# First causal attention of a four-layer kernel: where the row maximum gets its mask, and when the query and key stacks are turned and copied

## The chip, the cores and the metric

One core of one Trainium2 chip runs the whole program. The metric is the device time of one launch in microseconds (us), the median of several runs. Engines: PE (TensorE), DVE (VectorE), ACT (ScalarE), POOL (GpSimd), SP (DMA issue).

## The reference, cut to what matters

Four layers, each followed by a layer norm over 4 x 512 tokens of width 256. The change is in the first one alone:

```
Q = (x @ Wq.T).reshape(b, h, t, d)          # b 4, h 16, t 512, d 16
K = (x @ Wk.T).reshape(b, h, t, d)
V = (x @ Wv.T).reshape(b, h, t, d)
scores = einsum('bhqd,bhkd->bhqk', Q, K)
scores = where(causal, -inf, scores)        # causal: k > q
weights = softmax(scores / sqrt(d))
ctx = einsum('bhqk,bhkd->bhqd', weights, V) # then @ Wp.T + bp, + x, layer norm
```

Behind it come a gated mixture of eight experts, a second attention with 16 heads of width 128, and a routed feed-forward layer.

## The kernel before, in words

**Slots, groups, chunks.** The 64 heads (4 x 16) of the first attention are worked in 16 groups of four heads. A group `g` has two slots, `p = 2g` (even, `j = 0`) and `p = 2g + 1` (odd, `j = 1`), and a slot handles a pair of heads, one on partitions 0 to 63 and one on 64 to 127. Each engine walks the same list of slots (`l0_slot`, from -6 to 33), and each slot has three chunks. The order of the work on an engine is the order in which its `l0_slot` calls the helpers; semaphores tie the engines together. Nothing is planned at run time.

**Two passes over the scores.** The softmax needs the row maximum before the exponential. In the first pass (`l0_scores`, two slots ahead) PE multiplies queries by keys with query rows on the partitions, into banks 0 (first head) and 1 (second head), and DVE takes the row maximum of each row tile (`l0_maxima`, L1405 to L1416) into `nm0`. Chunk 0 is the row tile with 512 keys, chunk 1 the tiles with 384 and 128 keys in one bank, chunk 2 the tile with 256 keys; each for both heads. POOL splits the maxima into three bf16 parts (`l0_split_maxima`, L1925 to L1928), and PE folds them into the queries (`l0_row_maxima`, L544 and L547). In the second pass (`l0_turned_scores`, L563 the mask and L568 the scores, banks 3 to 5) the scores come out with the keys on the partitions and the maximum already taken off; ACT exponentiates them from PSUM (`l0_exponentials`, L1082), and PE multiplies by the values (`l0_context`, L584, bank 6), turns the result back (`l0_context_turns`, L593), and DVE copies it out (L1401).

**The mask of the first pass.** PE writes it: before the scores of a row tile, four 64-row matmuls (L526), two per head, put the 128 x 128 causal triangle (0 or -1e30, as identity times mask) on the diagonal block, and the score matmul (L531) adds to it. The first of them for a head waits on `a["max"]` until DVE has read what that bank held before.

**The stacks.** PE projects a group's queries and keys three groups ahead (`l0_project`, even slot, chunk 2, L457 to L459) and its values (`l0_values`, odd slot, chunk 2). ACT and DVE split queries and keys into bf16 parts (`l0_parts_high`, even slot, chunk 2; `l0_parts_low`, odd slot, chunk 0, L1356), POOL writes duplicates (L1893). Then PE turns both, one after the other, through bank 7: 32 transposes of 64 x 64 each (`l0_stack`, L507). The turned queries are copied to SBUF by ACT (`l0_q_stack`, L1063, a 128 x 1024 copy), the turned keys by DVE (`l0_k_stack`, L1384 to L1390, the same size). The turns of the keys wait for ACT's copy of the queries (`a["stq"]`), the next turns of queries for DVE's copy of the keys (`a["stk"]`). In the kernel before, the query turns are in chunk 1 of the even slot, the key turns in chunk 1 of the odd slot; ACT's copy is in chunk 1 of the even slot, DVE's in chunk 1 of the odd slot.

**The early work.** From slot 26 on, the tables `EARLY_AT` put the first steps of the next layer (`cc`, `first`, `join`, `norm`, `x1`) between the attention's own. Their turns (`turn_mix`, L648) use bank 7 too, so PE waits there for the stacks' copies.

`mask` is a 128 x 512 tile of constants: zeros, and the triangle in its last 128 columns, so that `mask[:, 512 - w:512]` is the mask of a row tile with `w` keys. The second attention's first pass already uses it in this way (`maxima`, L1418 to L1429): one DVE instruction adds the mask to the scores in PSUM, writes the sum to SBUF and takes the row extreme, and a second one reads the accumulator out.

Of the kernel before, what the change touches and what calls it, by code (L numbers as in the profile page):

```python
# [7 lines left out]
ALU = mybir.AluOpType  # L8
# [3 lines left out]
P = 128  # L12
# [134 lines left out]
def build(nc, x_tok_d, x_t_d, wqkv_d, wall_d, const_d, bp_d, outb_d, b2_d, rb_d, eb_d, rw0_d, rw1_d, b1_d, out_d):  # L147
    ctx = ExitStack()
    with ctx:
# [304 lines left out]
        def _(pe):  # L454
# [35 lines left out]
            def l0_stack(g, which):  # L490

                tok = (q_tok, k_tok)[which][g % 2]
                hold(pe, m["tlo"], sum(what in ("cc", "x1") for at in EARLY_AT if at < (2 * g - 4 + which, 1)
                                       for what, _ in EARLY_AT[at]))
                if which == 0:
                    hold(pe, a["stk"], g)
                    pe.wait_ge(a["plo"], 2 * g + 2)
                    pe.wait_ge(a["dup"], 2 * g + 2)
                    if is_first(g):
                        pe.wait_ge(z_ready, Z_ALL)  # L500
                        pe.wait_ge(c_ready, C_ALL)
                else:
                    pe.wait_ge(a["stq"], g + 1)
                out = bank[7][:, :].bitcast(BF16)
                for ch in range(HEADS):
                    for h in range(2):
                        last = pe.transpose(out[half(h), ch * ROWS:(ch + 1) * ROWS], tok[half(h), ch, :],  # L507
                                            ident_b[half(h), half(h)])
                last.then_inc(a[("tq", "tk")[which]], 1)

            def l0_scores(p, chunk):

                g, j = divmod(p, 2)
                if chunk == 0:
                    pe.wait_ge(a["stk"], g + 1)
                if p == 0 and chunk == 0:
                    pe.wait_ge(ld_s, 96)
                out = [bank[h] for h in range(2)]
                for i, (qt, col) in enumerate(S_CHUNKS[chunk]):
                    diagonal = col + qt * P  # L520
                    for part, first in enumerate((0, ROWS)):
                        for h in range(2):
                            if i == 0 and part == 0:
                                hold(pe, a["max"], 6 * p + 2 * chunk + h - 1)
                            moved = h != part
                            pe.matmul(out[h][:, diagonal + first:diagonal + P], (ident_b, ident_s)[moved][half(h), :],  # L526
                                      (mask_b, mask_s)[moved][half(h), first:P], start=(i == 0 and part == 0),
                                      stop=False, skip_group_check=True)
                    w = (qt + 1) * P
                    for h in range(2):  # L530
                        last = pe.matmul(out[h][:, col:col + w], q_stack[g % 2][half(h), ds(j * TOK + qt * P, P)],  # L531
                                         k_stack[g % 3][half(h), ds(j * TOK, w)], start=False, stop=True,
                                         skip_group_check=True)
                        if i == len(S_CHUNKS[chunk]) - 1:
                            last.then_inc(a["s"], 1)
# [60 lines left out]
            def l0_slot(p):  # L596
                g, j = divmod(p, 2)
                for chunk in range(3):
                    if 0 <= p + 2 < NP:
                        l0_scores(p + 2, chunk)  # L600
                    if 0 <= p < NP:
                        l0_turned_scores(p, chunk)
                    if chunk == 0 and j == 0 and 0 <= g - 1 < NT:
                        l0_context(g - 1, 2)
                    if chunk == 0 and 0 <= p + 1 < NP:
                        l0_row_maxima(p + 1)
                    if chunk == 1 and j == 0 and 0 <= g - 1 < NT:
                        l0_context_turns(g - 1)
                    if chunk == 1 and j == 1 and 0 <= g < NT:
                        l0_context(g, 0)  # L610
                    if chunk == 1 and 0 <= g + 2 < NT:
                        l0_stack(g + 2, j)
                    if chunk == 2 and 0 <= g + 3 < NT:
                        (l0_project, l0_values)[j](g + 3)
                    if chunk == 2 and j == 1 and 0 <= g < NT:
                        l0_context(g, 1)
                    for what, t in early(p, chunk):
                        if what in ("cc", "x1"):
                            if p < 30:
                                pe.wait_ge(a["stk"], NT if p > 27 else NT - 1)  # L620
                                pe.wait_ge(a["stq"], NT)
                            else:
                                pe.wait_ge(a["max"], 6 * NP)
                            turn_mix(what, t)
                        elif what == "first":
                            if t == 0:
                                pe.wait_ge(ch_done, 1)
                            pe.wait_ge(a["qt"], min(p + 2, NP))
                            first_project(t)
                        elif what == "logits":  # L630
                            logits(t)
# [402 lines left out]
        def _(act):  # L1034
# [65 lines left out]
            def l0_slot(p):  # L1100
                g, j = divmod(p, 2)
                for chunk in range(3):
                    if 0 <= p < NP:
                        l0_exponentials(p, chunk)
                    if chunk == 0 and j == 0 and 0 <= g - 1 < NT:
                        l0_context(g - 1)
                    if chunk == 0 and 0 <= p + 1 < NP:
                        l0_query_maxima(p + 1)
                    if chunk == 1 and j == 0 and 0 <= g + 2 < NT:
                        l0_q_stack(g + 2)  # L1110
                    if chunk == 2 and j == 0 and 0 <= g + 3 < NT:
                        l0_parts_high(g + 3)
                    for what, t in early(p, chunk):
                        if what in ("cc", "x1"):
                            turned_high(what, t)
                        elif what == "route":
                            router_exp(m, 1, slice(0, TT * NX))
# [236 lines left out]
        def _(dve):  # L1354
# [50 lines left out]
            def l0_maxima(p, chunk):  # L1405
# [3 lines left out]
                for h in range(2):  # L1409
                    n = 6 * p + 2 * chunk + h  # L1410
                    dve.wait_ge(a["s"], n + 1)
                    for qt, col in S_CHUNKS[chunk]:
                        w = (qt + 1) * P
                        last = dve.tensor_reduce(nm0[:, p % 2, h, qt:qt + 1], bank[n % 2][:, col:col + w], AX.X,  # L1414
                                                 ALU.max)
                    last.then_inc(a["max"], 1)  # L1416

            def maxima(s, g, j, chunk, scale):  # L1418
# [109 lines left out]
            def l0_slot(p):  # L1528
                g, j = divmod(p, 2)
                for chunk in range(3):  # L1530
                    if 0 <= p + 2 < NP:
                        l0_maxima(p + 2, chunk)
                    if chunk == 1 and j == 1 and 0 <= g + 2 < NT:
                        l0_k_stack(g + 2)
                    if chunk == 1 and j == 0 and 0 <= g - 1 < NT:
                        l0_context(g - 1)
# [605 lines left out]
```

## Time and profile before

| | |
|---|---|
| median of 3 runs | 917.42 us (914.79 to 920.34) |
| the profiled execution's own time | 918.97 us |
| its span | 917.2 us (1.77 us lie around it) |
| busy in the span | PE 90%, DVE 76%, PE weight loads 56%, ACT 54%, POOL 42% |
| mean granted clock of PE | 0.959 of full speed |
| the first attention | about 20 to 255 us of the span |

The engines' busy shares are means over all stages. A row of the trace gives the start and the duration of an instruction (or of several merged ones, with xN), its engine, its line in the kernel, and what it writes and reads. An engine's idle time stands behind it in brackets, with the instruction that ended it. Durations of matmuls overlap, since they are pipelined; what a matmul takes of PE's time is read from the distance between starts.

### The profile page before, as it was taken

Reading aid. Unit: us, or ns where it says so; the run is one execution under the profiler, and the core shown is the slowest. Engines: PE = TensorE matmul, PEld = TensorE weight load, DVE = VectorE, ACT = ScalarE, POOL = GpSimd, SP = SyncE. Lnnn points to the kernel's source line nnn. Section 1 sums busy time; section 2 is a strip of 40 time slices with the busy share of each in tenths; the row PEclk is TensorE's granted clock in tenths of the full one; section 3 lists DMA queues with packets and bytes.
Section 4 is the critical chain, followed back from the end, with each engine's and each line's share of the span. In section 5 each row is a group of like instructions: output and inputs, shape, how many; then the busy total and the mean of one; then the engine's idle time right before and its main releaser. Section 6 shows DMA issues by size and latency. Waiting matters only on the chain.

```text
span 917.2 us, 21939 instructions
## 1 busy us (share of the span) xinstructions
PE 824.4 (90%) x8101; PEld 517.6 (56%) x8197; DVE 699.6 (76%) x1945; ACT 496.7 (54%) x1181; POOL 389.2 (42%) x727
## 2 busy tenths in 40 slices
PE   5799999996779889879999999999999999996894
PEld 2455555553335445445565766666776676685364
DVE  3677777777568887758999888888888888866535
ACT  3377687775425355337676565655556655532143
POOL 4356456444426556433333333333333333333454
PEclk8799999999779999999999999999999999998897
DMA  7342233320000000004667756556555555560402
GB/s 267 86 107 61 81 94 71 95 31 8 1 1 1 1 1 1 1 1 88 115 122 124 113 96 106 92 102 98 98 109 99 95 105 94 100 102 1 92 1 93
DMA packets 218602, 67.70 MB, mean 74 GB/s; under 512 B 211312, under 2 KB 214656, under 8 KB 218368
## 3 DMA queue, kind: packets, MB, share of 16 engines
q1 hardware_dynamic: 218496, 66.29, 36.9%
q8 instruction: 66, 1.08, 0.5%
q14 instruction: 40, 0.33, 0.1%
HBM read 17.92 MB, written 4.19 MB: 24 GB/s over the span
## 4 chain that ended last, share of the span: by engine, by line
PE 69%; DVE 14%; issue 6%; DMA 4%; ACT 3%; POOL 3%; SPq 1%; POOLq 0%; DVEq 0%; ACTq 0%
PE bank L458 14%; PE bank L459 13%; PE bank L457 12%; PE bank L584 4%; PE bank L812 4%; PE bank L814 3%; PE bank L813 3%; DVE nm L1414 3%; DMA att<-w_lo 3%; PE bank L531 2%; PE bank L526 2%; PE bank L507 2%; DVE w_lo L1438 2%; PE bank L568 1%; DVE scr L1589 1%
## 5 line engine op out<-in xcount | busy, mean ns | idle before, releaser
L1131 ACT ACTIVATE att<-att,nm 128x512 f32<-128x512 f32 (+3 forms) x256 | 141.4, 553 | 103.8 <-DVE nm L1427 102.4
L1036 ACT ACTIVATE scr<-bank 128x512 bf16<-128x512 f32 (+3 forms) x210 | 111.6, 550 | 103.0 <-PE bank L814 43.7
L458 PE MATMUL bank<-w_lo,scr 128*128 128x256 bf16 (+1 forms) x478 | 145.6, 305 | 0.8 <-issue 0.4
L457 PE MATMUL bank<-w_hi,scr 128*128 128x256 bf16 (+1 forms) x471 | 142.8, 303 | 2.2 <-DVE scr L1356 2.0
L459 PE MATMUL bank<-w_hi,scr 128*128 128x256 bf16 (+1 forms) x476 | 144.6, 304 | 0.1
L1414 DVE TENSOR_REDUCE nm<-bank 128x1 f32<-128x512 f32 (+3 forms) x256 | 110.6, 484 | 40.4 <-PE bank L531 40.4
L1427 DVE CUSTOM_DVE_ANT_0 att<-bank,consts 128x512 f32<-128x512 f32 (+3 forms) x256 | 113.4, 483 | 15.0 <-PE bank L459 15.0
L2039 POOL TENSOR_SCALAR wqkv_hi<-att,rr 128x512 bf16<-128x512 f32 (+3 forms) x128 | 65.6, 531 | 137.2 <-DVE rr L1444 137.2
L1356 DVE TENSOR_TENSOR scr<-bank,scr 128x256 bf16<-128x256 f32 (+1 forms) x146 | 77.5, 541 | 56.9 <-ACT scr L1036 56.3
L1082 ACT ACTIVATE att<-bank 128x512 f32<-128x512 f32 (+1 forms) x192 | 90.8, 528 | 53.3 <-PE bank L568 53.0
L2039 POOL TENSOR_SCALAR w_hi<-att,rr 128x512 bf16<-128x512 f32 (+3 forms) x128 | 65.6, 532 | 106.6 <-DVE rr L1444 106.6
L812 PE MATMUL bank<-att,w_hi 128*128 128x384 bf16 (+2 forms) x320 | 84.0, 273 | 4.6 <-DMA att<-w_lo 3.8
L813 PE MATMUL bank<-att,w_hi 128*128 128x384 bf16 (+2 forms) x320 | 87.2, 273 | 0.0
L814 PE MATMUL bank<-att,w_lo 128*128 128x384 bf16 (+2 forms) x320 | 83.9, 273 | 0.0
L458 PE MATMUL bank<-w_lo,w_hi 128*128 128x512 bf16 (+3 forms) x256 | 76.6, 299 | 0.6 <-DVE w_lo L1356 0.6
L457 PE MATMUL bank<-w_hi 128*128 128x512 bf16 (+1 forms) x255 | 72.9, 299 | 0.0
L459 PE MATMUL bank<-w_hi,w_lo 128*128 128x384 bf16 (+1 forms) x255 | 72.9, 299 | 0.0
L1356 DVE TENSOR_TENSOR w_lo<-bank,w_hi 128x512 bf16<-128x512 f32 x96 | 66.4, 692 | 7.1 <-ACT w_hi L1036 6.5
L1163 ACT ACTIVATE scr<-bank 128x512 f32<-128x512 f32 x64 | 38.1, 597 | 59.3 <-PE bank L459 37.0
L1036 ACT ACTIVATE w_hi<-bank 128x512 bf16<-128x512 f32 x96 | 55.7, 582 | 25.3 <-PE bank L459 25.2
L458 PE MATMUL bank<-xt_lo,w_hi 128*128 128x512 bf16 x176 | 67.2, 382 | 2.5 <-issue 0.2
L459 PE MATMUL bank<-xt_hi,w_lo 128*128 128x512 bf16 x176 | 67.1, 381 | 0.0
(241 smaller groups left out, 2028.5 us busy)
## 6 DMA issues: line engine op xcount, KB each, us to landing
scr<-wall_in SPq DMA_DIRECT2D x19, 512.0 KB, 4.8
x_tok<-x_tok_in SPq DMA_DIRECT2D x1, 2048.0 KB, 12.1
v_by_token<-scr SPq DMA_DIRECT2D x16, 128.0 KB, 1.8
scr<-v_by_token SPq DMA_DIRECT2D x16, 128.0 KB, 3.2
scr<-x_t_in SPq DMA_DIRECT2D x3, 512.0 KB, 5.6
out<-x_tok SPq DMA_DIRECT2D x3, 512.0 KB, 2.6
scr<-wqkv_in SPq DMA_DIRECT2D x2, 384.0 KB, 3.5
att<-w_hi SPq DMA_TRANSPOSE x32, 3.4
```

Source lines behind the costliest of these rows:

```text
L457: pe.matmul(out, l_hi, r_hi, start=start, stop=False, skip_group_check=check)
L458: pe.matmul(out, l_hi, r_lo, start=False, stop=False, skip_group_check=check)
L459: return pe.matmul(out, l_lo, r_hi, start=False, stop=stop, skip_group_check=check)
L812: pe.matmul(out, v1_hi[:, vs], hi, start=(kt, q0) == (0, 0), stop=False, skip_group_check=True)
L813: pe.matmul(out, v1_hi[:, vs], lo, start=False, stop=False, skip_group_check=True)
L814: last = pe.matmul(out, v1_lo[:, vs], hi, start=False, stop=(kt == TT - 1), skip_group_check=True)
L1036: return act.activation(out, in_, ACT.Copy)
L1131: last = act.activation(at, at, ACT.Exp, bias=nm[:, j % 2, qt:qt + 1], scale=-1.0, accum_out=rs[:, j % 2, qt:qt + 1])
L1356: return dve.tensor_tensor(out, bank_cols, hi, ALU.subtract)
L1414: last = dve.tensor_reduce(nm0[:, p % 2, h, qt:qt + 1], bank[n % 2][:, col:col + w], AX.X, ALU.max)
L1427: last = dve.tensor_tensor_reduce(s_sb[j % 2][:, S_OFF[qt]:S_OFF[qt] + w], bank[turn][:, col:col + w], mask[:, 512 - w:512], -scale, HUGE, ...
L2039: pool.tensor_scalar(ps_hi[j % 2][:, at], s_sb[j % 2][:, at], rr[:, j % 2, qt:qt + 1], 1.0, ALU.mult, ALU.mult).then_inc(c["row"], 1)
```

## The change

PE no longer writes a mask in the first pass: the score matmuls open the bank's accumulation themselves, and the wait on `a["max"]` moves to them. DVE's `tensor_reduce` becomes a `tensor_tensor_reduce` that adds `mask` to the scores in the bank, writes the sum back to the same bank and takes the maximum. The mask of the second pass is left alone, and so is everything that builds and moves the constants.

The turns of the queries move to chunk 0 and those of the keys to chunk 1 of the even slot; ACT's copy moves to chunk 0 of the even slot, DVE's copy to chunk 2 of the even slot. So all turns are issued before the first early turn, and a wait of `l0_stack` on the early turns goes; the early turns of slots 26 to 29 now wait for the last group's key copy.

```diff
@@ -490,8 +490,6 @@
             def l0_stack(g, which):
 
                 tok = (q_tok, k_tok)[which][g % 2]
-                hold(pe, m["tlo"], sum(what in ("cc", "x1") for at in EARLY_AT if at < (2 * g - 4 + which, 1)
-                                       for what, _ in EARLY_AT[at]))
                 if which == 0:
                     hold(pe, a["stk"], g)
                     pe.wait_ge(a["plo"], 2 * g + 2)
@@ -517,19 +515,12 @@
                     pe.wait_ge(ld_s, 96)
                 out = [bank[h] for h in range(2)]
                 for i, (qt, col) in enumerate(S_CHUNKS[chunk]):
-                    diagonal = col + qt * P
-                    for part, first in enumerate((0, ROWS)):
-                        for h in range(2):
-                            if i == 0 and part == 0:
-                                hold(pe, a["max"], 6 * p + 2 * chunk + h - 1)
-                            moved = h != part
-                            pe.matmul(out[h][:, diagonal + first:diagonal + P], (ident_b, ident_s)[moved][half(h), :],
-                                      (mask_b, mask_s)[moved][half(h), first:P], start=(i == 0 and part == 0),
-                                      stop=False, skip_group_check=True)
                     w = (qt + 1) * P
                     for h in range(2):
+                        if i == 0:
+                            hold(pe, a["max"], 6 * p + 2 * chunk + h - 1)
                         last = pe.matmul(out[h][:, col:col + w], q_stack[g % 2][half(h), ds(j * TOK + qt * P, P)],
-                                         k_stack[g % 3][half(h), ds(j * TOK, w)], start=False, stop=True,
+                                         k_stack[g % 3][half(h), ds(j * TOK, w)], start=(i == 0), stop=True,
                                          skip_group_check=True)
                         if i == len(S_CHUNKS[chunk]) - 1:
                             last.then_inc(a["s"], 1)
@@ -608,8 +599,8 @@
                         l0_context_turns(g - 1)
                     if chunk == 1 and j == 1 and 0 <= g < NT:
                         l0_context(g, 0)
-                    if chunk == 1 and 0 <= g + 2 < NT:
-                        l0_stack(g + 2, j)
+                    if chunk < 2 and j == 0 and 0 <= g + 2 < NT:
+                        l0_stack(g + 2, chunk)
                     if chunk == 2 and 0 <= g + 3 < NT:
                         (l0_project, l0_values)[j](g + 3)
                     if chunk == 2 and j == 1 and 0 <= g < NT:
@@ -617,8 +608,7 @@
                     for what, t in early(p, chunk):
                         if what in ("cc", "x1"):
                             if p < 30:
-                                pe.wait_ge(a["stk"], NT if p > 27 else NT - 1)
-                                pe.wait_ge(a["stq"], NT)
+                                pe.wait_ge(a["stk"], NT)
                             else:
                                 pe.wait_ge(a["max"], 6 * NP)
                             turn_mix(what, t)
@@ -1106,7 +1096,7 @@
                         l0_context(g - 1)
                     if chunk == 0 and 0 <= p + 1 < NP:
                         l0_query_maxima(p + 1)
-                    if chunk == 1 and j == 0 and 0 <= g + 2 < NT:
+                    if chunk == 0 and j == 0 and 0 <= g + 2 < NT:
                         l0_q_stack(g + 2)
                     if chunk == 2 and j == 0 and 0 <= g + 3 < NT:
                         l0_parts_high(g + 3)
@@ -1411,8 +1401,9 @@
                     dve.wait_ge(a["s"], n + 1)
                     for qt, col in S_CHUNKS[chunk]:
                         w = (qt + 1) * P
-                        last = dve.tensor_reduce(nm0[:, p % 2, h, qt:qt + 1], bank[n % 2][:, col:col + w], AX.X,
-                                                 ALU.max)
+                        scores = bank[n % 2][:, col:col + w]
+                        last = dve.tensor_tensor_reduce(scores, scores, mask[:, 512 - w:512], 1.0, -HUGE, ALU.add,
+                                                        ALU.max, nm0[:, p % 2, h, qt:qt + 1])
                     last.then_inc(a["max"], 1)
 
             def maxima(s, g, j, chunk, scale):
@@ -1530,7 +1521,7 @@
                 for chunk in range(3):
                     if 0 <= p + 2 < NP:
                         l0_maxima(p + 2, chunk)
-                    if chunk == 1 and j == 1 and 0 <= g + 2 < NT:
+                    if chunk == 2 and j == 0 and 0 <= g + 2 < NT:
                         l0_k_stack(g + 2)
                     if chunk == 1 and j == 0 and 0 <= g - 1 < NT:
                         l0_context(g - 1)
```

## Rows read from the trace of the kernel before

**Rows 1.** The page: busy us, share of the span and instructions of the engines.

```profile
PE 824.4 (90%) x8101; PEld 517.6 (56%) x8197; DVE 699.6 (76%) x1945; ACT 496.7 (54%) x1181; POOL 389.2 (42%) x727
```

**Rows 2.** Busy by stretch; columns after the engines: granted clock, DMA share, GB/s.

```profile
46.00:207.00 161.00, 151.63 (x2785) 87.70 (x2810) 120.53 (x272) 118.92 (x240) 87.14 (x158) 1.00 0.34 77
207.00:230.00 23.00, 15.82 (x238) 9.19 (x245) 16.62 (x42) 11.73 (x27) 9.40 (x19) 0.95 0.07 8
```

**Rows 3.** Chain of waits, first and last of 13 even slots' row-maxima matmuls.

```profile
52.42 0.39 PE bank L547 x4
...
203.24 0.39 PE bank L547 x4
```

**Rows 4.** Timeline of PE, even slot 20, start of 21: start us, us, instruction.

```profile
164.05 0.23 PE L526 MATMUL bank<-past,ident_b 64*128 64x128 bf16 x1
...
165.86 0.23 PE L526 MATMUL bank<-past,ident_b 64*128 64x128 bf16 x1
165.98 0.23 PE L526 MATMUL bank<-past,scr 64*128 64x128 bf16 x2
...
168.07 0.23 PE L526 MATMUL bank<-past,ident_b 64*128 64x128 bf16 x1
...
169.97 0.23 PE L526 MATMUL bank<-past,ident_b 64*128 64x128 bf16 x1
```

**Rows 5.** Timeline of PE, odd slot 19.

```profile
157.40 0.23 PE L526 MATMUL bank<-past,ident_b 64*128 64x128 bf16 x1
...
157.49 0.38 PE L531 MATMUL bank<-scr 64*128 64x512 bf16 x2
...
158.72 0.23 PE L526 MATMUL bank<-past,ident_b 64*128 64x128 bf16 x1
159.32 0.23 PE L526 MATMUL bank<-past,scr 64*128 64x128 bf16 x2 [0.37 <-DVE nm L1414]
...
161.18 0.69 PE L507 MATMUL bank<-ident_b,scr 64*64 64x64 bf16 x32
161.81 0.23 PE L526 MATMUL bank<-past,ident_b 64*128 64x128 bf16 x1
```

**Rows 6.** Timeline of DVE, odd slot 19.

```profile
157.97 1.29 DVE L1414 TENSOR_REDUCE nm<-bank 128x1 f32<-128x512 f32 x2 [1.31 <-PE bank L531]
159.18 0.75 DVE L1356 TENSOR_TENSOR scr<-bank,scr 128x256 bf16<-128x256 f32 x2
159.87 1.42 DVE L1414 TENSOR_REDUCE nm<-bank 128x1 f32<-128x384 f32 x4
161.98 1.22 DVE L1388 COPY scr<-bank 128x1024 bf16<-128x1024 bf16 x1 [0.69 <-PE bank L507]
```

**Rows 7.** Groups by line and form: busy us, mean ns; L1414 in 0 to 460, L1427 in 440 to 810 us.

```profile
L1414 DVE TENSOR_REDUCE nm<-bank 128x1 f32<-128x512 f32 x64 | 41.2, 686 | 27.2 <-PE bank L531 27.2
...
L1427 DVE CUSTOM_DVE_ANT_0 att<-bank,consts 128x512 f32<-128x512 f32 x59 | 40.2, 681 | 0.0
...
L1427 DVE DVE_READ_ACCUMULATOR2_ANT nm<- 128x1 f32 x233 | 19.4, 83 | 0.0
```

**Rows 8.** Timeline of DVE in the second attention, one chunk of masked maxima.

```profile
559.45 0.55 DVE L1427 CUSTOM_DVE_ANT_0 att<-bank,consts 128x384 f32<-128x384 f32 x1
559.93 0.08 DVE L1427 DVE_READ_ACCUMULATOR2_ANT nm<- 128x1 f32 x1
559.93 0.29 DVE L1427 CUSTOM_DVE_ANT_0 att<-bank,consts 128x128 f32<-128x128 f32 x1
```

**Rows 9.** Timeline of ACT, even slot 20.

```profile
166.97 1.09 ACT L1082 ACTIVATE att<-bank 128x512 f32<-128x512 f32 x2
168.24 1.02 ACT L1036 ACTIVATE scr<-bank 128x1024 bf16<-128x1024 bf16 x1 [0.18 <-PE bank L507]
```

**Rows 10.** Timeline around slot 26: the first early turn, and DVE's work.

```profile
207.46 0.41 PE L648 MATMUL bank<-consts,scr 128*128 128x128 f32 x2 [1.13 <-DVE scr L1468]
...
207.23 0.75 DVE L1414 TENSOR_REDUCE nm<-bank 128x1 f32<-128x256 f32 x2
```

## The prediction

> **What bounds the kernel now.** I read the page first: PE is busy 90% of the span, DVE 76% [rows 1]. That is a mean over four layers, so I went to the stage that is changed. The table by stretch says that from 46 to 207 us, the steady part of the first attention, PE is busy 151.63 of 161 us at full granted clock, and DVE 120.53 [rows 2]. The chain of waits runs through PE there and repeats itself exactly: the row-maxima matmul of the even slot comes 13 times from 52.42 to 203.24 us, 12 periods of 12.57 us for a group of two slots [rows 3]. So a microsecond per group counts 13 times (slots 0 to 25), and the question is what a group costs.
>
> The timelines show it. The even slot runs from 164.05 to 169.97, 5.92 us, with one small wait of 0.12 us (165.86 to 165.98) [rows 4]. The odd slot runs from 157.40 to 164.05, 6.65 us [rows 4, 5]. In it PE stands still once: after row maxima it wants the banks of chunk 1 at about 158.6, and the second head's bank comes free at 159.32, when DVE is through with its two 512-wide maxima (157.97 + 1.29 = 159.26, so 0.06 us from DVE's end to PE's start) [rows 5, 6]. Otherwise PE is full, and DVE waits for PE (1.31 us, 0.69 us) [rows 6]. PE bounds both slots, DVE is close behind it in the odd one.
>
> **What goes: PE's masks.** The four mask matmuls of a row tile start at 157.40 and its scores at 157.49: 0.09 us a set, since the four overlap [rows 5]. The busy sums of such short overlapping matmuls would give several times as much. Four row tiles make 0.36 us a slot, 0.72 us a group, 11.5 us over 16 groups: the most that the edit can give by itself.
>
> **What comes: the mask in DVE's pass.** No row shows a DVE instruction that writes PSUM. The nearest is L1427, which reads the same operands and writes SBUF: 681 ns at 512 columns against 686 for the plain maximum, and an accumulator read of 83 ns on top [rows 7]. But that read is hidden: the pass of 384 columns starts at 559.45, its read at 559.93, and the next pass at 559.93 too, 0.07 us before the first has ended [rows 8]. The plain maxima overlap in the same way: two of 512 take 1.21 us to the next start (157.97 to 159.18) and not 1.37 [rows 6]. So I take no change per pass. The bounds: nothing gained (the pass has to stream the same columns); at worst, short of a conflict in the bank, the read's 0.08 us unhidden on each of the 16 passes of a group.
>
> The skill speaks against this. In the Trainium skill, "VectorE: DVE Perf Modes", section "The DRAIN you can't avoid" has the next operation wait until the pipe is empty, which would put each accumulator read behind its pass; this case's rows show the read starting 0.07 us before the end [rows 8]. Its section on two Vector instructions with no wait between them lets an instruction overlap unless start quadrants change, and here they do not. By the first rule the time would be the first rival's, by the second my forecast's.
>
> **What moves, even slot.** It gains the key turns, 0.63 us (161.18 to 161.81) [rows 5]. They wait for ACT's copy of the queries. ACT is through with chunk 0's exponentials, the context copy and the query copy at 166.97, where chunk 1's exponentials start at once [rows 9]; all of that comes 0.09 earlier, and the 1.02 us copy [rows 9] now stands there: ready at 166.88 + 1.02 + 0.05 = 167.95. PE leaves row maxima at 165.77, does the query turns (0.63) to 166.40, then chunk 1 and the context's turns, which took 165.86 to 168.07 less the 0.63 of turns, 1.58 us [rows 4], less two masks (0.18) and the 0.12 wait, which the query turns now cover: 167.68. So a wait of 0.27. Even slot: 5.92 - 0.36 - 0.12 + 0.63 + 0.27 = 6.34 us. Chunk 1's exponentials come about 1 us later on ACT, and the second pass of chunk 2 needs one of their banks at about 168.8; the first is done at 168.4, so this is covered, barely. POOL's duplicates and DVE's low parts are made in the odd slot before, microseconds ahead, and no DMA issue of SP is moved past anything.
>
> **What moves, odd slot.** It loses the 0.63 of turns, the 0.36 of masks and DVE's key copy of 1.22 us [rows 6]. PE's own work falls to about 5.1 us, and now DVE sets the pace. Counted from the slot's first score: DVE starts 0.48 later (157.49 to 157.97), two passes 1.21, the low parts 0.69 (159.18 to 159.87), four passes 1.42 [rows 5, 6], and 0.06 to PE: the bank for chunk 2's second head is free at 3.86 us. Before, the key turns lay in front of chunk 2 and hid this; now PE waits there some 0.35 us as well as 0.6 at chunk 1. From that score to the slot's end it was 161.90 to 164.05, 2.15 us [rows 4, 5]. Odd slot: 6.01 us. The key copy must be out of DVE's way first: scores of chunk 2 at 168.59, passes 0.67 to 0.75, copy 1.22, end at 170.7 to 171.0, against 170.88 where DVE is wanted; 0 to 0.16 us late, I take 0.
>
> A group becomes 6.34 + 6.01 = 12.35, 0.22 us less than 12.57: **of the 0.72 us, 0.50 go into new waits** of PE for DVE and ACT. Over 13 groups -2.9 us.
>
> **The ends.** In slots 26 to 33 PE no longer is full (15.82 of 23 us at clock 0.95) [rows 2]; its masks give perhaps 0.5 us there and in the first slots, of at most 0.36 x 6 = 2.2. Against this, the first early turn now waits for the last key copy. It started at 207.46, released by DVE [rows 10]; now DVE first does chunk 2's maxima from 207.23, 0.75 us, and the copy, 1.22: 209.2, 1.7 us later [rows 6, 10]. Slot 27 gets back the copy's place on DVE, so of this I count 1.2 us (bounds 0.5 and 1.7). The work of these slots is one chain across PE, ACT, DVE and POOL, so it arrives at the end of the layer. The granted clock in the steady part is 1.00 with PE busy 94%, and still 0.95 at 69% [rows 2]; with 1.2 us of waits in 12.35 I expect no loss.
>
> **Sum:** -2.9 - 0.5 + 1.2 = -2.2 us on the profiled execution's 918.97, 916.8. The median of the runs is 917.42, 1.55 lower; on that footing about **915.0 us**. A measurement of this kernel can tell about 0.5% (4.6 us) from no change, so this is within it.
>
> **Rivals.**
> 1. *The pass on DVE costs its accumulator read* (slower). Place: the twelve DVE passes from chunk 1 of the even slot to chunk 2 of the odd one, with the key copy among them, on which PE now waits. Price: 0.08 each, 0.96 us a group, less about 0.2 of slack, 0.75; a group then takes 13.1. It decides from 0.03 us a pass on, where the gain is gone. 13 x (0.75 - 0.22) = 6.9, the ends 0.7 and a further 1: +8.6, 926 us. For it: a write to PSUM is untried here. Against: the rows of L1427 [rows 8].
> 2. *The waits do not grow* (more gained). If moving the key copy off the odd slot lets DVE run ahead, PE keeps the whole 0.72: 13 x 0.72 = 9.4, less the ends' 0.7: 908.7 us. For it: DVE is busy only 75% of the stage [rows 2]. Against: the odd slot's 3.86 us, in which there is no room.
> 3. *Reading and writing one bank halves the pass.* Rows give 0.26 us for 256 columns (0.55 - 0.29) [rows 8]; 2560 columns a slot once more are 2.7 us, 5.3 a group, on top of DVE's 9.4 of 12.57. A group of at least 14.7, likely more: some +50 us, 967. No row speaks for it.
> 4. *The change does nothing*: if PE's masks lay wholly in its waits. Only those of the odd slot's chunk 1 do, so this is the forecast's upper edge, 917 us.
>
> **Chances.** Forecast with its edges 0.50, rival 1 0.22, rival 2 0.20, rival 3 0.05, rival 4 0.03. Faster by over 0.5% (under 912.8): rival 2 and a tenth from the forecast, 0.30. Slower by over 0.5% (over 922): rivals 3 and most of 1, 0.26. Within: 0.44. The range goes from 907 to 927, which leaves out rival 3 and the far ends of 1 and 2; the forecast alone would span 911 to 919.
>
> **What would show it.** In the profile after: no L526; the period of the even slot's row maxima near 12.35 us (12.57 before, 11.85 for rival 2, 13.1 for rival 1); two passes of 512 taking 1.2 us to the next start; a PE wait for DVE at the scores of chunk 2 of the odd slot, and one for ACT at the key turns; the first early turn about 1.7 us late against its slot. Wrong would be: accumulator reads that start after their pass has ended, DVE passes longer than 0.69 us at 512 columns, or a PE that waits for nothing in the odd slot.

## The result, and the profile after

The changed kernel takes 921.34 us in the median of 16 runs, against 917.25 of the kernel before: a ratio of 1.0048, 95% interval 1.0034 to 1.0063, **4.4 us slower** (3.1 to 5.8). One of the 16 runs of the kernel before took 2097 us and has no part in the ratio. A second series on another occasion, c1_after below, gave 1.0084 (1.0068 to 1.0100). I had forecast 2.2 us less. The time lies inside my range, 907 to 927, but on the other side of no change. 0.48% is also just under the 0.5% that I had called the least a measurement of this kernel can tell, so by itself it is a small loss; the interval and the profile make it a real one.

The page of the changed kernel, its engines (columns as in [rows 1]), and from the table by stretch the two stretches of [rows 2]:

```profile
PE 821.8 (89%) x7590; PEld 505.7 (55%) x7685; DVE 713.3 (77%) x2201; ACT 495.7 (54%) x1181; POOL 388.6 (42%) x727
```

```profile
46.00:207.00 161.00, 148.82 (x2373) 77.92 (x2398) 129.50 (x475) 117.76 (x240) 87.21 (x158) 1.00 0.32 73
207.00:230.00 23.00, 15.49 (x136) 7.07 (x138) 16.34 (x56) 9.80 (x22) 7.51 (x13) 0.78 0.07 7
```

PE has 511 matmuls fewer, and is busy 2.8 us less in the steady part; DVE is busy 9 us more there. The clock says more: 0.78 instead of 0.95 in the stretch after 207 us.

The row-maxima matmuls of PE's timeline serve as landmarks. They come once a slot, so the differences between them place the loss. Times in us from one profiled execution each, two for the kernel before and the changed one (c0_before and c1_after are the same kernels run again):

| from row maxima to row maxima | before | c0_before | changed | c1_after |
|---|---|---|---|---|
| slot 2 to slot 26 (12 groups) | 150.82 | 150.79 | 151.01 | 150.98 |
| slot 26 to slot 28 | 14.65 | 14.64 | 19.46 | 18.47 |
| slot 28 to slot 30 | 19.73 | 19.86 | 19.72 | 19.99 |
| start to slot 2 | 52.42 | 49.71 | 51.90 | 51.08 |

**The steady part brings 0.2 us of loss instead of 2.6 of gain over these 12 groups, and slots 26 and 27 cost 3.8 to 4.8 us.** What lies behind slot 30 varies by up to 6 us between profiles of like kernels (679.3 and 675.0 us for the changed one), and the start by up to 3, so a single profile's total says little here.

### The steady part

PE in an odd slot of the changed kernel (the view of [rows 5]): first scores, scores of chunk 2, and the first scores of slots 20 and 21.

```profile
157.45 0.39 PE L522 MATMUL bank<-scr 64*128 64x512 bf16 x2
...
161.25 0.64 PE L522 MATMUL bank<-scr 64*128 64x256 bf16 x2
...
163.76 0.39 PE L522 MATMUL bank<-scr 64*128 64x512 bf16 x2
...
170.04 0.39 PE L522 MATMUL bank<-scr 64*128 64x512 bf16 x2
```

The odd slot takes 163.76 - 157.45 = 6.31 us, the even one 6.28: 12.59, against 12.57 before and 12.35 forecast. The even slot is within 0.06 of the forecast. In the odd slot the first head's scores of chunk 2 start at 161.25 and the second's at about 161.61 (161.25 + 0.64 less the 0.28 that such a matmul takes), 4.16 us after the slot's first score, where I had 3.86. From there to the end it is 2.15 us, as forecast. So the slot is paced by DVE as I said. Of the 0.30 us, 0.25 come from DVE's passes and 0.06 from DVE's start, which is now 0.54 us after the slot's first score (157.99) and not 0.48; that part e5 below has too. DVE in the same slot (the view of [rows 6]):

```profile
157.99 0.70 DVE L1405 CUSTOM_DVE_ANT_0 bank<-bank,consts 128x512 f32<-128x512 f32 x1
158.60 0.14 DVE L1405 DVE_READ_ACCUMULATOR2_ANT nm<- 128x1 f32 x1
158.60 0.73 DVE L1405 CUSTOM_DVE_ANT_0 bank<-bank,consts 128x512 f32<-128x512 f32 x1
...
159.92 0.56 DVE L1405 CUSTOM_DVE_ANT_0 bank<-bank,consts 128x384 f32<-128x384 f32 x1
...
161.40 0.14 DVE L1405 DVE_READ_ACCUMULATOR2_ANT nm<- 128x1 f32 x1
```

And the groups by form, changed kernel, 0 to 460 us (the view of [rows 7]):

```profile
L1405 DVE CUSTOM_DVE_ANT_0 bank<-bank,consts 128x512 f32<-128x512 f32 x64 | 43.1, 715 | 18.0 <-PE bank L522 16.8
...
L1405 DVE DVE_READ_ACCUMULATOR2_ANT nm<- 128x1 f32 x256 | 36.3, 142 | 0.0
```

The read still starts together with the next pass (158.60), so it does not hold that pass up. The Trainium skill, "VectorE: DVE Perf Modes", section "The DRAIN you can't avoid", has the next operation wait until the pipe is empty, and says that one that is not held back starts earlier; the trace shows the second case. But with the bank as output the pass is 715 ns and not 681, the read 142 and not 83, and two passes of 512 columns take 1.26 us to the next start (157.99 to 159.25), where two plain maxima took 1.21. The last read of a chunk has no pass behind it to hide it: it starts before its pass, which began at 161.15, ends (161.40, against 161.15 + 0.33 = 161.48) and ends 0.06 us after it, at 161.54, and PE's scores come at 161.61. So the four passes of chunk 1 take 161.54 - 159.92 = 1.62 us, 1.42 before.

### Slots 26 and 27

The changed kernel around its first early turn (the view of [rows 10]), PE, then DVE, then POOL:

```profile
206.15 0.30 PE L559 MATMUL bank<-scr 64*128 64x256 bf16 x2
209.45 0.69 PE L638 MATMUL bank<-consts,scr 128*128 128x128 f32 x2 [3.00 <-DVE scr L1378]
```

```profile
208.18 1.22 DVE L1378 COPY scr<-bank 128x1024 bf16<-128x1024 bf16 x1
...
210.93 1.10 DVE L1459 TENSOR_TENSOR scr<-scr 128x256 f32<-128x256 f32 x1
```

```profile
209.41 2.35 POOL L1925 TENSOR_TENSOR x_tok<-x_tok,bp_bc 128x1024 f32<-128x1024 f32 x1
```

Three things are to be seen. PE waits 3.00 us for the last key copy; the turn comes 6.54 us after the slot's row maxima (202.91) against 4.22 before (203.24 to 207.46). Then PE's turn itself takes 0.69 us, not 0.41: the clock has fallen. And DVE's context product, 0.42 us when alone, takes 1.10, beside POOL's bias addition. The table by stretch for the clock, changed kernel and then the kernel before:

```profile
209.00:212.00 3.00, 2.22 (x14) 1.12 (x15) 1.80 (x4) 1.02 (x3) 2.67 (x3) 0.50 0.01 2
212.00:215.00 3.00, 2.85 (x25) 1.51 (x26) 3.00 (x12) 1.46 (x4) 0.00 (x0) 0.50 0.00 1
215.00:218.00 3.00, 3.00 (x24) 0.64 (x20) 1.47 (x8) 1.45 (x4) 0.10 (x1) 0.50 0.00 0
```

```profile
209.00:212.00 3.00, 2.43 (x38) 1.46 (x39) 2.36 (x6) 2.48 (x6) 2.46 (x2) 1.00 0.01 2
```

For these 9 us the granted clock is 0.50, the lower of its two levels, 1.2 GHz; in the kernel before it is 1.00.

### The profile page after: what moved, and what is told of

Same layout as the page of the kernel before. It is cut to its first block, busy times and chain, and to the rows that moved or that the text cites. A ratio compares the mean times of both kernels' runs of the same rounds, so it can differ in the third digit from the quotient of the medians.

```text
span 921.4 us, 21166 instructions
## 1 busy us (share of the span) xinstructions
PE 821.8 (89%) x7590; PEld 505.7 (55%) x7685; DVE 713.3 (77%) x2201; ACT 495.7 (54%) x1181; POOL 388.6 (42%) x727
## 4 chain that ended last, share of the span: by engine, by line
PE 59%; DVE 18%; issue 7%; ACT 6%; DMA 4%; POOL 4%; SPq 1%; POOLq 0%; DVEq 0%; ACTq 0%
PE bank L458 14%; PE bank L459 13%; PE bank L457 12%; DVE bank L1405 5%; PE bank L802 4%; PE bank L804 3%; PE bank L803 3%; DMA att<-w_lo 3%; ACT scr L1026 3%; PE bank L575 2%; DVE w_lo L1429 2%; DVE scr L1346 2%; PE bank L522 2%; ACT att L1072 1%; DVE scr L1580 1%
## 5 line engine op out<-in xcount | busy, mean ns | idle before, releaser
L1405 DVE CUSTOM_DVE_ANT_0 bank<-bank,consts 128x512 f32<-128x512 f32 (+3 forms) x256 | 119.6, 518 | 33.5 <-PE bank L522 31.2
L1346 DVE TENSOR_TENSOR scr<-bank,scr 128x256 bf16<-128x256 f32 (+1 forms) x146 | 77.5, 541 | 53.7 <-ACT scr L1026 53.4
```

Of the source, the lines that this page charges most:

```text
L1346: return dve.tensor_tensor(out, bank_cols, hi, ALU.subtract)
L1405: last = dve.tensor_tensor_reduce(scores, scores, mask[:, 512 - w:512], 1.0, -HUGE, ALU.add, ALU.max, nm0[:, p % 2, h, qt:qt + 1])
```

## The experiments

Each was run beside the kernel before; the ratio is to it, over the runs of that occasion. The landmarks of all of them, in us (steady: the mean group between row maxima of slot 2 and of slot 22). The last column is the time that the clock spent at its lower level in the 20 us behind the row maxima of slot 26, and in the 14 us behind those, added up from tables by stretch of 0.5 us:

| kernel | ratio (95%) | steady group | slot 26 to 28 | slot 28 to 30 | lower clock, 0 to 20; 20 to 34 |
|---|---|---|---|---|---|
| before, c0_before | 1.0011 (0.9990 to 1.0032) | 12.57 | 14.65, 14.64 | 19.73, 19.86 | 0, 0; 3.4, 3.4 |
| changed, c1_after | 1.0048 (1.0034 to 1.0063), 1.0084 (1.0068 to 1.0100) | 12.58 | 19.46, 18.47 | 19.72, 19.99 | 10.2, 6.8; 3.4, 3.4 |
| e1_mask_only | 1.0019 (1.0000 to 1.0038) | 12.45 | 15.67 | 20.76 | 3.4; 10.2 |
| e2_stack_only | 1.0054 (1.0032 to 1.0077) | 12.62 | 17.11 | 19.58 | 3.4; 3.4 |
| e3_other_bank | 1.0066 (1.0042 to 1.0090) | 12.58 | 18.57 | 19.87 | 6.8; 3.4 |
| e4_fill | 1.0081 (1.0056 to 1.0106) | 12.58 | 17.35 | 20.53 | 0; 10.2 |
| e5_sbuf_out | 1.0021 (1.0005 to 1.0036) | 12.36 | 17.37 | 19.76 | 3.4; 3.4 |
| e6_bank_bias | 1.0034 (1.0014 to 1.0053) | 12.58 | 15.56 | 19.69 | 0.3; 3.1 |
| e7_last_old | 1.0038 (1.0019 to 1.0057) | 12.58 | 15.58 | 19.69 | 3.4; 3.4 |
| e8_mask_bias | 0.9995 (0.9976 to 1.0014) | 12.45 | 15.70 | 19.85 | 3.4; 3.4 |
| e9_before_bias | 0.9999 (0.9977 to 1.0021) | 12.57 | 14.58 | 19.74 | 0; 3.4 |
| e10_mask_sbuf_bias | 0.9972 (0.9949 to 0.9995) | 12.19 | 15.03 | 20.08 | 0; 3.4 |
| e11_changed_bias | 1.0053 (1.0027 to 1.0079) | 12.58 | 18.26 | 19.60 | 6.8; 3.4 |
| e12_fill_bias | 1.0039 (1.0014 to 1.0063) | 12.58 | 16.62 | 20.01 | 0; 6.8 |

### One part alone

**e1_mask_only**: the diff's hunks for `l0_scores` and `l0_maxima` alone, on the kernel before.

> The mask goes into VectorE's maximum, the turns and copies stay where they were before. Theory A (the change's 4 us come from slots 26 and 27, where PE waits 3.0 us for the last key copy and its clock then falls to half): no such wait here, so at worst the time of before; the group's period falls from 12.57 to about 12.3 us, and the time is near 914 us against 917.3 of before. Theory B (the dearer passes on VectorE, 715 ns and a 142 ns read, are what costs): as slow as the changed kernel, 919 to 922 us.

Measured: 917.5 us, 1.0019, between the two theories (914, and 919 to 922). The group falls to 12.45 us and the 3.0 us wait is absent; but slot 26 to 28 takes 15.67 us, a microsecond more than before, and slot 28 to 30 another 1.0. The dearer passes are only a part of it, for the clock fell here too, without a long wait (PE's longest in front of it is 1.23 us), and again from 221 us on. e8 and e10 below have the same code in these slots, and take 15.70 and 15.03 us; the table by stretch for e8, then e10, from 6 us behind the row maxima of slot 26:

```profile
205.50:208.50 3.00, 2.33 (x26) 1.60 (x31) 1.87 (x7) 1.55 (x4) 0.23 (x1) 0.59 0.03 7
```

```profile
201.70:204.70 3.00, 2.37 (x32) 1.37 (x35) 2.18 (x7) 2.48 (x6) 0.23 (x1) 1.00 0.03 7
```

So the passes cost 0.4 us there at full clock (14.65 to 15.03), and the other 0.7 us of e8 go with 3.4 us at the lower clock.

**e2_stack_only**: the rest of the diff alone.

> PE writes the mask as before, the turns and copies are moved. Theory A: the wait for the last key copy and the fall of the clock are here too, +4.5 us in slots 26 and 27, and the steady period is about 12.6 to 12.7 us: 921 to 924 us. Theory B: VectorE's passes are the old ones, so the time of before, 917 us, or less.

Measured: 921.57 us, 1.0054, a group of 12.62 us, 17.11 us from slot 26 to 28. So most of the loss comes with the move of the stacks, with no changed pass on DVE (wait 2.87 us, context product 1.29 us, 3.4 us at the lower clock). The rival that the dearer passes alone cost the 4 us has fallen. The move costs the steady part a little as well: 12.57 to 12.62 here, and 12.45 to 12.58 from e1 to the changed kernel.

### Taking the wait away

**e3_other_bank**: the first early turn goes to bank 2.

```diff
         def turn_bank(i):
-            return 7 if i < LONE_TURNS else i % 2
+            return 2 if i == 0 else 7 if i < LONE_TURNS else i % 2
...
-                            if p < 30:
+                            if (what, t) == TURNS[0]:
+                                pe.wait_ge(a["qt"], p + 2)
+                            elif p < 30:
                                 pe.wait_ge(a["stk"], NT)
...
                 hold(pe, a["qt"], p)
+                hold(pe, m["tlo"], int(p == 28))
```

> The changed kernel, but the first early turn writes bank 2 instead of bank 7, so it need not wait for the last key copy; the row maxima of slot 27 wait until that bank is read. Theory A: no long wait, granted clock 1.00 from 206 to 221 us, and 4 to 4.5 us less than the changed kernel: 917 us, equal to before. Theory B: under 1 us gained, 920 to 921 us.

Measured: 922.0 us, 1.0066. A miss: the wait for the copy went (1.23 us, for the context, in place of 3.00), and nothing was gained. DVE and POOL of this kernel show why:

```profile
208.27 2.39 DVE L1462 TENSOR_TENSOR scr<-scr 128x256 f32<-128x256 f32 x1
```

```profile
208.04 2.34 POOL L1928 TENSOR_TENSOR x_tok<-x_tok,bp_bc 128x1024 f32<-128x1024 f32 x1
```

The context product, now earlier, met POOL's bias addition at its start. It ended 0.28 us after that addition (210.66 and 210.38); in the changed kernel too (212.03 and 211.76, 0.27). Its length is therefore set by when it meets the addition: 2.39 us here, 1.10 in the changed kernel, 0.42 free. Both instructions read two operands in SBUF. The Trainium skill, "SBUF — State Buffer", section "Who interferes with whom", says that a VectorE instruction with two SBUF inputs contends with a GpSimd instruction that reads SBUF; the rows agree, and put the price at the whole of what is left of POOL's instruction. The clock was at 0.50 from 209 to 215 us here as well.

**e6_bank_bias**: e3, and POOL's first addition moves out of the way.

```diff
-                if p in BIAS_SLOTS:
-                    add_bias(p - BIAS_SLOTS[0])
+                if p in (26, 28, 29, 30):
+                    add_bias(max(p - BIAS_SLOTS[0], 0))
```

> As e3_other_bank (first early turn in bank 2, 922.0 us), and POOL's first bias addition of 2.35 us comes in slot 26, where POOL is idle, not in slot 27, where it ran beside VectorE's context product of slot 26, which then took 2.39 us instead of 0.42. Theory A (slots 26 and 27 cost the change its 4 us, by the wait and by this collision behind it): 5 us less than e3, about 916 to 917 us. Theory B (the loss lies elsewhere): within 1 us of e3.

Measured: 917.63 us, 1.0034, 4.4 us less than c1_after on the same occasion (e3 ran on another; by the ratios e6 is 2.9 us below it, and the intervals overlap). The granted clock is 1.00 through to 221 us, and slot 26 to slot 28 takes 15.56 us: 0.5 more than e10, which has the stacks at their old places and the clock at 1.00 too. The first early turn still comes 4.76 us after the row maxima of slot 26, not 4.22. The control for it:

**e9_before_bias**: POOL's edit alone, on the kernel before.

> The kernel before with nothing but POOL's first bias addition in slot 26. Its context product was stretched by 0.07 us only, so the time of before, 0.998 to 1.001; it tells what of the 4.4 us between e3_other_bank and e6_bank_bias is a gain that the kernel before could have too.

Measured: 0.9999. So the collision is none of the kernel before's, and what e6 gives back is a cost of the change.

**e7_last_old**: the changed kernel, with the last group's stacks, copies and waits in their old places.

```diff
+                if g == NT - 1:
+                    hold(pe, m["tlo"], 2 * which)
...
+                    if g + 2 == NT - 1:
+                        if chunk == 1:
+                            l0_stack(g + 2, j)
-                    if chunk < 2 and j == 0 and 0 <= g + 2 < NT:
+                    elif chunk < 2 and j == 0 and 0 <= g + 2 < NT:
...
-                                pe.wait_ge(a["stk"], NT)
+                                pe.wait_ge(a["stk"], NT if p > 27 else NT - 1)
+                                pe.wait_ge(a["stq"], NT)
```

> The changed kernel, but the last group's stacks are turned and copied where they were before, so that slots 26 and 27 are as before except for the mask. Theory A: the 4 us are gone, 1.000 of before. Theory B: as the changed kernel, 1.005 of before.

Measured: 918.38 us, 1.0038, and 15.58 us from slot 26 to 28, 2.9 to 3.9 less than the changed kernel of the two profiles. On this occasion c1_after stood at 922.04, so one group's stacks give back 3.7 us of 6.7. Not all: the ratio of 1.000 that I expected is outside the interval.

### The copy of the changed kernel, and where its 4 us divide

**c1_after**: the changed kernel again.

> The changed kernel once more, beside the next three: 1.0048 of before again, and in its profile again some 4 to 5 us more than before between the row maxima of slot 26 and those of slot 30, none in the steady part. If the clock's fall there was chance, those 4 us are 2 to 3 in this profile and the steady part or the start has the rest.

Measured: 1.0084; the landmarks repeat (table). The clock fell in this profile too, to 0.54 and 0.50 from 209 to 215 us, but for 6.8 us and not 10.2, and slot 26 to 28 is 1.0 us shorter. So much of the changed kernel's 4.8 us varies from one execution to the next with the length of the fall.

**e4_fill**: PE is kept busy in the wait.

```diff
+                            if (what, t) == TURNS[0]:
+                                pe.wait_ge(a["qt"], p + 2)
+                                for _ in range(14):
+                                    pe.matmul(bank[2][:, :], ident_b[:, :], xt_hi[:, 0, 0:TOK], start=True,
+                                              stop=True, skip_group_check=True)
```

> The changed kernel, with 14 matmuls of 512 columns in front of the wait for the last key copy, into a bank that nobody reads then: PE is busy in the wait, which stays. If the fall of the clock behind the wait costs 2.5 us of the 4.5, as theory A has it: granted clock 1.00 from 209 to 221 us, 2 to 2.5 us less than the changed kernel, 919 us. If the wait alone costs them: 921 to 922 us, the matmuls bringing nothing. They are left out of the result.

Measured: granted clock 1.00 from 206 to 221 us, slot 26 to 28 in 17.35 us, 1.1 to 2.1 less than the changed kernel; but 922.58 us, no gain in the median. The collision was in it (1.36 us), and the fall of the clock came later instead: 10.2 us at the lower level between 20 and 34 us behind the row maxima, where the changed kernel has 3.4. Slot 28 to 30 took 20.53 us, 0.5 to 0.8 more, so up to slot 30 only 0.6 to 1.3 us were gained. What gave back the rest is not shown.

**e11_changed_bias**: the collision alone taken away (POOL's edit of e6 on the changed kernel). **e12_fill_bias**: e4 with it.

> The changed kernel with POOL's first bias addition in slot 26 and the wait for the last key copy left as it is. The context product of slot 27 (1.10 and 1.36 us in two profiles of the changed kernel) falls to 0.42; the wait of 3.0 us and the clock's fall stay. From the row maxima of slot 26 to those of slot 30: 37.5 to 38.3 us, against 38.5 and 39.2 of the changed kernel and 34.4 of before; a ratio of about 1.005. If the collision is all of it, 35.3 us and 1.002.

> e4_fill with the bias addition in slot 26: the wait stays, the clock is kept, the collision is gone. What is left is the wait: 36.3 to 37 us from the row maxima of slot 26 to those of slot 30. If the clock's fall costs nothing of its own, the same as e11.

Measured: 1.0053 and 1.0039; slot 26 to 28 in 18.26 and 16.62 us. The context product was 0.41 us in both. From the row maxima of slot 26 to those of slot 30 they took 37.86 and 36.63 us, both as expected. The table by stretch of e12, to be read against the first row of the changed kernel:

```profile
209.00:212.00 3.00, 2.77 (x22) 1.16 (x19) 2.06 (x6) 1.47 (x4) 0.64 (x3) 1.00 0.01 1
```

Read in order, the 14.65 us of before, from slot 26 to 28, grow

- to 15.03 by the dearer passes (e10),
- to 15.56 by the moved stacks, without the wait and the collision (e6),
- to 16.62 with the wait (e12),
- to 18.26 with 6.8 us at the lower clock (e11),
- to 18.47 with the collision and the same 6.8 us (c1_after), and to 19.46 with 10.2 us at the lower clock (changed).

That is **0.4 + 0.5 + 1.1 + 1.6 + 0.2 us, and 1.0 more in the one profile with the longer fall**. At full clock the collision costs 0.7 us (e12 to e4). Each step rests on one profile of each kernel; the runs of e11 and e12 do not decide it: the ratios are 1.3 us apart with intervals of 2 us on either side, and the medians 0.2 us the other way (920.07 and 920.31). The step of the clock is 1.2 us and not 1.6 when counted up to slot 30, because the clock of e12 falls later and for longer (6.8 us against 3.4 between 20 and 34 us).

The wait of 3.0 us is not the whole condition for the fall. e1, e7 and e8 spent 3.4 us at the lower level there with no wait over 1.3 us, and e10 and the kernel before none, with waits no longer. e3, whose clock fell 7 us behind the row maxima with no wait over 1.3 us up to then, spent 6.8 us there, and e2 and e5, with waits of 2.87 and 3.00 us, only 3.4. What decides between them no run here shows.

### What the pass costs, and whether it can pay

**e5_sbuf_out**: the sum goes to SBUF up to pair 24.

```diff
+                        lows = w_lo[:, (17 + n % 2) * CH:(18 + n % 2) * CH].bitcast(F32)
+                        out = lows[:, col:col + w] if p < 25 else scores
-                        last = dve.tensor_tensor_reduce(scores, scores, mask[:, 512 - w:512], 1.0, -HUGE, ALU.add,
+                        last = dve.tensor_tensor_reduce(out, scores, mask[:, 512 - w:512], 1.0, -HUGE, ALU.add,
```

> The changed kernel, but up to pair 24 the masked pass writes its sum into SBUF (weights not yet loaded there) and not back to the bank; nobody reads it in either. If the write to PSUM is what makes a pass dearer: 681 ns and a read of 83 ns instead of 715 and 142 in the steady part, its period 0.3 us shorter, 12.3 instead of 12.6 us, and 3 to 4 us less than the changed kernel. If the price is that of the operation, or the odd slot is not bound by VectorE: no difference.

Measured (groups by form of e5, 46 to 170 us):

```profile
L1407 DVE CUSTOM_DVE_ANT_0 w_lo<-bank,consts 128x512 f32<-128x512 f32 x40 | 26.1, 689 | 10.4 <-PE bank L522 9.2
...
L1407 DVE DVE_READ_ACCUMULATOR2_ANT nm<- 128x1 f32 x160 | 13.2, 83 | 0.0
```

689 and 83 ns, a group of 12.36 us, 0.22 less than with PSUM as output. The group is my forecast's to 0.01 us, and in part by luck: its odd slot takes 6.10 us (forecast 6.01), its even one 6.26 (6.34). So what the pass costs more than forecast is the price of its output, not of the operation. The median is 916.47 us, 5.6 less than the changed kernel on the same occasion, and the passes account for less than half: 2.3 us from slot 2 to slot 26. Another 1.1 to 2.1 us come from slot 26 to 28, where e5's code is the changed kernel's and the clock was at its lower level for 3.4 us only.

**e8_mask_bias** and **e10_mask_sbuf_bias**: e1 with POOL's edit; and that with e5's edit.

> Mask in VectorE's pass, turns and copies as before (e1_mask_only, 1.0019), and POOL's first bias addition in slot 26. If that addition's collision with VectorE costs in e1 too, 1 us less than e1; the context product there took 0.48 us, 0.06 more than alone, so I expect less than 1 us, a ratio of 1.000.

> e8_mask_bias with the masked pass writing SBUF up to pair 24. With PSUM output a group took 12.45 us in e1; the cheaper pass took 0.23 off in e5, so about 12.2 us here, 3 us less than e8: 912 to 914 us, under the kernel before. If PE bounds the group without the new waits, under 1 us less than e8.

Measured: 0.9995 and 0.9972, a group of 12.45 and 12.19 us. e10 is the only version below the kernel before by more than its interval, 913.7 us against 916.5: the mask on DVE with its sum in SBUF, the stacks where they were. It is 0.3%, less than the 0.5% set as the measure of a clear gain.

**c0_before**: the kernel before against itself.

> The kernel before against itself: ratio 1.000, which shows how far the interval can be trusted, and a second profile of it. If the first profile was an ordinary one, 150.8 us from the row maxima of slot 2 to those of slot 26 and 34.4 from there to slot 30 come again, within 0.3 and 1 us.

Measured: 1.0011 (0.9990 to 1.0032), landmarks within 0.15 us. A microsecond between two ratios says nothing; and the two series of the changed kernel, 1.0048 and 1.0084, lie 3.3 us apart with intervals that do not meet, so ratios from different occasions tell less than their intervals say.

## Why the prediction was wrong, point by point

- **PE bounds the steady part, the odd slot goes over to DVE, most of the mask's gain turns into waits**: right. With the price that I had for a pass, e5 gives 12.36 us a group against 12.35 forecast, though its two slots are off by +0.09 and -0.08. In the changed kernel the even slot takes 6.28 us against 6.34, and the odd slot's second half 2.15 as forecast.
- **"So I take no change per pass"**: the first step that failed. I took L1427's price, whose output is SBUF. With PSUM it is 34 ns more a pass of 512 columns and 59 ns more a read, 0.22 us a group (e5), and that is all of the steady gain: +0.2 us where I had -2.6 over the 12 groups between the landmarks (-2.9 over 13). My first rival had the place right (DVE's chain through the odd slot) and the mechanism mostly wrong: the reads are hidden behind the next pass, and only the last one of a chunk shows, by 0.06 us. The point where it decides, 0.03 us a pass, was right, and the measured price sits on it. A pass that writes where no row has it written needed this as its middle case, not as a bound.
- **"Of this I count 1.2 us"**: the second step, and the larger. The first turn's delay was 2.3 us against its slot (I had 1.7), but what followed it was not in the sum: slots 26 and 27 together lost 3.8 to 4.8 us, of which the fall of the clock is, by the steps above, 1.6 (c1_after) to 2.6 (changed).
- **"I expect no loss" of clock**: wrong in its place. I judged the steady part, where it is right (1.00), and from the mean of a stretch. The changed kernel has PE stand still for 3.0 us in one piece behind a stretch that is thin already. The kernel before shows the same: 3.15 us of PE waiting for POOL up to 227.21 us, with the clock at 0.65 in the 3 us behind it. I had read that row, and did not ask what a wait of 3 us would do earlier. But the fall in e1, e7 and e8, without such a wait, shows that this row would not have been enough to forecast it.
- **POOL's queue**: I wrote that POOL's work of the moved steps was microseconds ahead, and named no instruction of another engine that DVE's delayed ones would run beside. Moved by 2 us, the context product met the bias addition, for 0.2 us (e11 to c1_after) to 0.7 us (e12 to e4).
- **The 0.5 us for masks at the ends**: the sign was wrong; with the pass writing PSUM, slots 26 and 27 lose 0.4 us by the masks' move at full clock (e10), and 1.0 where the clock falls for 3.4 us (e1, e8).
- **Two slips in the sums**: 916.8 less 1.55 is 915.2 us and not 915.0, and rival 3's 2560 columns at 0.26 us for 256 are 2.6 us and not 2.7. Neither changes anything.
- **Still open**: e6 and e7, in which slots 26 and 27 have neither the wait nor the collision, stand at 1.0034 and 1.0038, 3 us, where their landmarks from slot 2 to slot 30 give 1.0 us over the kernel before. The intervals are 2 us wide on either side. Part may lie in the first slots, where the moved stacks begin: the start to slot 2 took 49.6 to 53.7 us, 51.4 in the mean, in the ten profiles with them and 49.1 to 52.4, 50.3 in the mean, in the six others, too spread to be sure of. No run took that part by itself.

## What to carry to other kernels

A wait moved in front of the first instruction of a chain can cost more than its length: look for the longest single standstill of PE that the change creates, for the clock behind it, and for what runs on the neighbour engine at the time to which the delayed work moves. Read the granted clock beside every landmark before putting a difference down to an instruction: e8 and e10 have the same code in slots 26 and 27 and are 0.7 us apart there. A price taken from an instruction of the same kind is good only where its output goes to the same memory. And when an experiment takes the suspected wait away and nothing is gained, look at what the freed instruction now meets before dropping the theory: e3 alone would have acquitted the wait.

## What the runs showed of the hardware that I had not expected

- VectorE's masked maximum with its output in PSUM: 715 ns at 512 columns and an accumulator read of 142 ns, against 689 and 83 with SBUF as output and the same inputs (e5).
- VectorE's 128x256 f32 product of two SBUF operands waits out a GpSimd addition of 128x1024 f32: 2.39 us instead of 0.42, ending 0.28 us after it.
- TensorE's granted clock stood at 0.50 for 10.2, 6.8 and 3.4 us behind a standstill of 3.0 us (changed, c1_after, e5), and at 1.00 up to 221 us when that standstill was filled with matmuls (e4, e12); but it fell later there, for 10.2 and 6.8 us where the changed kernel has 3.4. In e1, e7 and e8 it fell for 3.4 us, and in e3 for 6.8, behind no wait over 1.3 us.
